# A feed-forward turn in another order: the route at its head, and the last of five chunks in fp32 in the second product

## What is computed

```python
        x_mixed = _mix(x, mix_kernel)
        h = jnp.einsum('bsd,pdm->bspm', x_mixed, W1) + b1
        stacked_paths = jnp.einsum('bspm,pmd->bspd', h, W2) + b2
        scores = jnp.tanh(x_mixed @ Wo1 + bo1) @ Wo2 + bo2
        idx = jnp.argmax(scores, axis=-1)
        weights = jax.nn.one_hot(idx, P, dtype=stacked_paths.dtype)
        collapsed = jnp.einsum('bspd,bsp->bsd', stacked_paths, weights)
        return _layernorm(x + collapsed, gamma, beta)
    ...
    x = x + 0.5 * _L0_ffn_ref(_layernorm(x, axis=-1), ...)
    x = x + _L0_attn_ref(_layernorm(x, axis=-1), ...)
    x = x + 0.5 * _L0_ffn_ref(_layernorm(x, axis=-1), ...)
```

## Time and profile before

| | |
|---|---|
| median of 3 runs | 1528.1 us (1524.33 to 1539.24) |
| the profiled execution | 1531.81 us, span 1530.0 us |
| busy share of the span | PE 89%, DVE 79%, ACT 61%, POOL 20% |
| phase 0, attention, phase 1 | about 0 to 340, 340 to 1220, 1220 to 1530 us |
| DMA | 82.26 MB, mean 54 GB/s |

### The profile page before, as it was taken

How to read it: one execution, slowest core, us unless ns; L and a number is a source line. 1 busy time by engine, 2 the same in 40 slices (tenths; PEclk the granted TensorE clock), 3 DMA queues, 4 the chain that set the end, 5 groups by cost and what they waited for, 6 DMA issues and landing times.

```text
span 1530.0 us, 25980 instructions
## 1 busy us (share of the span) xinstructions
PE 1359.1 (89%) x7700; PEld 781.4 (51%) x7700; DVE 1215.7 (79%) x2349; ACT 936.8 (61%) x1745; POOL 306.9 (20%) x359
## 2 busy tenths in 40 slices
PE   4889988858999999999968999999998779989985
PEld 2556666544554454545344455454444346656653
DVE  6989999766677677677866767777678769999985
ACT  5656665326567666566855666766666666666642
POOL 2244452332001000000041101000000214444311
PEclk9989999979999999999989999999999879999997
DMA  5143333320000100102110011000103112333221
GB/s 155 43 118 88 90 101 113 90 69 1 28 29 15 41 14 15 32 11 74 37 43 1 28 42 42 0 28 0 42 0 110 56 32 61 103 97 106 61 74 57
DMA packets 86994, 82.26 MB, mean 54 GB/s; under 512 B 8540, under 2 KB 86885, under 8 KB 86885
## 3 DMA queue, kind: packets, MB, share of 16 engines
q1 hardware_dynamic: 86884, 80.91, 17.8%
HBM read 55.43 MB, written 25.46 MB: 53 GB/s over the span
## 4 chain that ended last, share of the span: by engine, by line
PE 62%; DVE 11%; DMA 10%; issue 7%; ACT 6%; SPq 2%; POOL 1%; DVEq 0%; ACTq 0%; POOLq 0%
PE PS L1324 55%; DMA R<-oh_scratch 7%; PE PS L1501 3%; DMA oh_scratch<-oh_t 2%; DVE R L753 2%; PE PS L1389 2%; PE PS L1332 1%; DVE R L770 1%; DVE R L937 1%; SPq L414 1%; SPq L412 1%; ACT oh_t L1113 1%; ACT R L1211 1%; ACT R L1215 1%; ACT R L1174 1%
## 5 line engine op out<-in xcount | busy, mean ns | idle before, releaser
L1324 PE MATMUL PS<-R 128*128 128x512 f16 (+3 forms) x3456 | 713.6, 361 | 27.4 <-DVE R L937 17.3
L1324 PEld LDWEIGHTS PS<-R 128*128 128x128 f16 (+1 forms) x3456 | 326.0, 98 | 392.3 <-DVE R L937 32.0
L1324 PE MATMUL PS<-w_hi,R 128*128 128x256 f16 x1280 | 239.1, 280 | 63.3 <-DVE R L753 63.1
L937 DVE TENSOR_TENSOR R<-R 128x512 f16<-128x512 f32 (+3 forms) x288 | 188.6, 655 | 111.5 <-ACT R L1215 110.3
L1202 ACT ACTIVATE R<-PS 128x512 f32 (+5 forms) x288 | 160.2, 558 | 162.7 <-PE PS L1324 162.2
L1324 PE MATMUL PS<-R,w_hi 128*128 128x512 f16 x640 | 198.0, 392 | 1.6 <-DVE R L747 1.5
L1211 ACT ACTIVATE R<-R 128x512 f32 (+4 forms) x288 | 169.5, 589 | 48.3 <-DVE R L931 46.8
L931 DVE TENSOR_TENSOR R<-R,max_row 128x512 f32 (+4 forms) x288 | 187.1, 650 | 7.7 <-ACT max_row L1248 7.7
L1215 ACT ACTIVATE R<-R 128x512 f16<-128x512 f32 (+3 forms) x288 | 171.1, 594 | 28.6 <-ACT R L1211 2.6
L925 DVE TENSOR_TENSOR run_max<-run_max,R 128x512 f32<-128x512 f32 (+3 forms) x272 | 173.9, 639 | 10.0 <-DVE run_max L925 1.7
L1324 PEld LDWEIGHTS PS<-w_hi,R 128*128 128x128 f16 x1280 | 128.4, 100 | 104.5 <-DVE R L753 77.1
(11 more groups left out here) (109 smaller groups left out, 1555.3 us busy)
## 6 DMA issues: line engine op xcount, KB each, us to landing
R<-x_scratch SPq DMA_DIRECT2D x48, 512.0 KB, 4.5
x_scratch<-R SPq DMA_DIRECT2D x32, 512.0 KB, 3.2
R<-oh_scratch SPq DMA_DIRECT2D x32, 320.0 KB
R<-in_L_attn_x SPq DMA_DIRECT2D x16, 512.0 KB, 5.4
R<-oh_scratch SPq DMA_DIRECT2D x32, 256.0 KB
out<-R SPq DMA_DIRECT2D x16, 512.0 KB, 3.2
R<-in_L_ffn_W SPq DMA_DIRECT2D x2, 288.0 KB
R<-in_L_ffn_W SPq DMA_DIRECT2D x1, 512.0 KB
```

The lines of the kernel that those rows point to most:

```text
L937: v.tensor_tensor(p_lo[:, i * TT + lo:(i + 1) * TT], pf[:, (i % 2) * TT + lo:(i % 2 + 1) * TT], p_hi[:, i * TT + lo:(i + 1) * TT], ALU.sub ...
L1324: ins = t_.matmul(dst, w, xx, start=start and n == 0, stop=stop and n == last, skip_group_check=skip)
```

## The change

- DVE's turn begins with result(t-1) and then the five route steps of tile t+2, with the four bn_stats of tile t+6 placed between them (input_sums becomes input_sum, one bn_stats at a time; the wait for x_in is at the first). The mix and the moments come next, then the masks.
- PE's turn begins with the route's scores; choice comes behind path 0. Chunk 0 of tile t+3 (FIRST = 3) is made near the end of the turn, behind transposed(t+5) and ahead of path 4, where it was chunk 0 of t+2 at the turn's head. ACT's turn begins with scores and has one_hot earlier.
- The last chunk (LAST = 4) is no longer split for the second product (w2_last is written in prepare_second, w2_hi and w2_lo shrink to four chunks): masked_high 2 on ACT and masked_low 2 on DVE go, and path(t, 4) multiplies the fp32 masks by fp32 weights (w2_last), four matmuls of 256 columns in place of twelve in f16. hm has two places for chunk 4; hhi and hlo have four chunks.
- POOL's residual moves from tile t+1 behind the masks to tile t behind o_psum of the tile before, at the head of POOL's turn; result_scale(t-1) moves to its end.
- mask_in becomes two semaphores, one for even and one for odd tiles. SP's order of transfers in a turn stays as it is.

```diff
@@ -36,8 +36,12 @@
 
 STATS, ROWS, MIX, ROUTE, HIDDEN = 6, 5, 3, 2, 1
 
-GROUPS = ((0, 2), (2, 2), (4, 1))
-GROUP_OF = (0, 0, 1, 1, 2)
+FIRST = ROUTE + 1
+
+GROUPS = ((0, 2), (2, 2))
+GROUP_OF = (0, 0, 1, 1)
+LAST = HC - 1
+
 XBUF = 3
...
@@ -345,14 +350,22 @@
         h_order = []
         for ph in range(2):
             for t in turns():
-                h_order += [(use(ph, t + ROUTE), 0)] if on(t + ROUTE) else []
                 h_order += [(use(ph, t + HIDDEN), c) for c in range(1, HC)] if on(t + HIDDEN) else []
+                h_order += [(use(ph, t + FIRST), 0)] if on(t + FIRST) else []
         h_bank = {x: i % H_BANKS for i, x in enumerate(h_order)}
         h_before = {x: h_order[i - H_BANKS] if i >= H_BANKS else None for i, x in enumerate(h_order)}
...
+
+        def masked_chunk(t, c, n=1):
+
+            return cols(hm, (c + (t % 2 if c == LAST else 0)) * TT, n * TT)
...
@@ -549,15 +562,14 @@
                     if ph == 0 and t == 0:
                         pool.wait_ge(w2_ready, 1)
                     pool.wait_ge(n_done, k + 1)
-                    pool.wait_ge(hm_done, HC * k + 4)
+                    if t >= 1:
+                        pool.wait_ge(o_psum, k)
                     g.tensor_tensor(rows4(x_rows(t)), rows4(x_rows(t)),
                                     beta_b[:, :].unsqueeze(1).to_broadcast([P, SUB, D]), ALU.add).then_inc(xb_done, 1)
 
                 def turn(t):
-                    if on(t - 1):
-                        result_scale(t - 1)
-                    if on(t + HIDDEN):
-                        residual(t + HIDDEN)
+                    if on(t):
...
@@ -566,6 +578,8 @@
                                    (n_var, n_eps, n_rstd, n_neg, n_shift))
                     elif first_of(ph, t):
                         first_scales(0, first_of(ph, t))
+                    if on(t - 1):
+                        result_scale(t - 1)
 
...
@@ -716,12 +732,15 @@
                 v.memset(chunk(mask, 1, 0)[0:DM, :], 0.0).then_inc(edges_set, 1)
                 dve.wait_ge(edges_set, ph + 1)
 
-                def input_sums(t):
+                def input_sum(t, u):
                     n = counted(ph, t)
-                    dve.wait_ge(x_in[t % NT], 16 * loads(ph, t))
-                    if n >= 2:
-                        dve.wait_ge(n_shift, n - 1)
-                    row_sums(X, t % NT * SUB * D, rows_set(ph, t), n_stat)
+                    if u == 0:
+                        dve.wait_ge(x_in[t % NT], 16 * loads(ph, t))
+                        if n >= 2:
+                            dve.wait_ge(n_shift, n - 1)
+                    ins = v.bn_stats(st[:, rows_set(ph, t), u, :], cols(x_rows(t), u * D, D))
+                    if u == SUB - 1:
+                        ins.then_inc(n_stat, 1)
 
...
@@ -793,11 +812,13 @@
                 def masked(t, c):
 
                     g = use(ph, t)
-                    at = cols(hm, c * TT, TT)
-                    if c in (0, 2, 4) and g >= 1:
-                        dve.wait_ge(hlo_done, 3 * (g - 1) + GROUP_OF[c] + 1)
+                    at = masked_chunk(t, c)
+                    if c in (0, 2) and g >= 1:
+                        dve.wait_ge(hlo_done, len(GROUPS) * (g - 1) + GROUP_OF[c] + 1)
+                    if c == LAST and g >= 2:
+                        dve.wait_ge(o_psum, g - 1)
                     if c == 0:
-                        dve.wait_ge(mask_in, 16 * MASK_LOADS * (g + 1))
+                        dve.wait_ge(mask_in[g % 2], 16 * MASK_LOADS * (g // 2 + 1))
                         dve.wait_ge(hb_done, g + 1)
...
@@ -818,48 +840,34 @@
                         prepare_first()
                     if last:
                         result(t - 1)
+                    for i in range(SUB + 1):
+                        if choice:
+                            route(t + ROUTE, i)
+                        if rows and i < SUB:
+                            input_sum(t + STATS, i)
+                    if mix:
+                        mixed_before(t + MIX, 0)
+                        mixed_before(t + MIX, 1)
+                    if rows:
+                        input_moments(t + STATS)
+                    elif first_of(ph, t):
+                        first_stats(0, first_of(ph, t))
+                    if mix:
+                        mixed_behind(t + MIX, 0)
+                        mixed_behind(t + MIX, 1)
                     if here:
                         masked(t + HIDDEN, 0)
                         masked(t + HIDDEN, 1)
                     if mix:
-                        mixed_before(t + MIX, 0)
-                        mixed_before(t + MIX, 1)
-                    if choice:
-                        route(t + ROUTE, 0)
+                        mixed_low(t + MIX)
                     if here:
                         masked_low(t + HIDDEN, 0)
-                    if choice:
-                        route(t + ROUTE, 1)
-                    if here:
                         masked(t + HIDDEN, 2)
-                    if choice:
-                        route(t + ROUTE, 2)
-                    if mix:
-                        mixed_behind(t + MIX, 0)
-                    if choice:
-                        route(t + ROUTE, 3)
-                    if mix:
-                        mixed_behind(t + MIX, 1)
-                    if choice:
-                        route(t + ROUTE, 4)
-                    if here:
                         masked(t + HIDDEN, 3)
-                    if rows:
-                        input_sums(t + STATS)
-                    elif first_of(ph, t):
-                        first_stats(0, first_of(ph, t))
-                    if mix:
-                        mixed_low(t + MIX)
-                    if here:
                         masked(t + HIDDEN, 4)
-                    if rows:
-                        input_moments(t + STATS)
-                    if here:
                         masked_low(t + HIDDEN, 1)
                     if last:
                         result_scaled(t - 1)
-                    if here:
-                        masked_low(t + HIDDEN, 2)
                     if last:
                         result_added(t - 1)
                     if ph == 0 and t == -ROUTE:
...
@@ -1135,26 +1143,23 @@
                         act.wait_ge(kmix_ready, 1)
                     if ph == 0 and t == -ROUTE:
                         act.wait_ge(w1_ready, 1)
+                    if choice:
+                        scores(t + ROUTE)
                     if mix:
                         middle(t + MIX)
-                    if choice:
-                        scores(t + ROUTE)
-                    if here:
-                        masked_high(t + HIDDEN, 0)
                     if last:
                         squares(t - 1)
+                    if choice:
+                        one_hot(t + ROUTE)
                     if on(t + ROWS):
                         normalised(t + ROWS)
                     if mix:
                         x_high(t + MIX)
-                    if choice:
-                        one_hot(t + ROUTE)
                     if here:
+                        masked_high(t + HIDDEN, 0)
                         masked_high(t + HIDDEN, 1)
                     if on(t + ROWS):
                         transposed(t + ROWS)
-                    if here:
-                        masked_high(t + HIDDEN, 2)
 
                 for t in turns():
...
@@ -1402,29 +1407,35 @@
                     g = use(ph, t)
                     if c == 0 and g >= 1:
                         pe.wait_ge(y_done, g)
-                    pe.wait_ge(hlo_done, 3 * g + GROUP_OF[c] + 1)
-                    high, low = chunk(hhi, t, c), chunk(hlo, t, c)
+                    if c == LAST:
+                        pe.wait_ge(hm_done, HC * g + HC)
+                        rows, w = masked_chunk(t, c), w2_last[:, :]
+                    else:
+                        pe.wait_ge(hlo_done, len(GROUPS) * g + GROUP_OF[c] + 1)
+                        high, low = split_chunk(hhi, t, c), split_chunk(hlo, t, c)
                     for u in range(SUB):
-                        ins = split_product(ps_o[:, u // 2, (u % 2) * D:(u % 2 + 1) * D],
-                                            [((cols(high, u * P, P), cols(low, u * P, P)), (w2_hi[:, c, :], w2_lo[:, c, :]))],
-                                            c == 0 and u % 2 == 0, c == HC - 1, skip=True)
+                        dst = ps_o[:, u // 2, (u % 2) * D:(u % 2 + 1) * D]
+                        if c == LAST:
+                            ins = t_.matmul(dst, cols(rows, u * P, P), w, start=False, stop=True, skip_group_check=True)
+                        else:
+                            ins = split_product(dst, [((cols(high, u * P, P), cols(low, u * P, P)),
+                                                       (w2_hi[:, c, :], w2_lo[:, c, :]))],
+                                                c == 0 and u % 2 == 0, False, skip=True)
```

(23 more changed lines are left out.)

37 lines of the change are left out of this document (22 added, 15 removed).

## The result

The changed kernel takes 1590.67 us (median of 4 runs, 1588.00 to 1593.52) beside 1526.21 us for the one before (4 runs). The ratio is 1.0404, 95% interval 1.0342 to 1.0466: slower, as predicted, but by 64 us between the medians (some 62 by the ratio) instead of 31, and above the upper end of the range (1588). The profiled execution took 1591.11 us with a span of 1589.3, against the 1530.0 of before: +59.3.

What follows compares the result with a forecast made beforehand. DVE was taken as the bound, busy 17.12 of 17.20 us a turn. For each phase +25.1 for loaded turns and -9.4 elsewhere made +15.7, +31.4 for both, so about 1559 us from 1528.1; range 1541 to 1588.

Steps and rivals of the forecast that it cites:

- The load at the head of the turn: In turns 2 to 9 DVE's first bn_stats waits 4.0 us for the rows' load: +25.1 us for each phase.
- the wait of 0.6 for ACT: On DVE between masked 4 and masked_low 1: 0.6 us stay open while it waits for ACT's copy.
- The price of 20.3: Length of a loaded turn, taken between alternating turns of 20.9 and 19.8 us; eight make 162.4 against 137.3 us.
- The clock: PE's clock falls to 0.50 for 5.0 us behind a 3.88 us gap, losing 2.5 us, in every other loaded turn.
- The rival built on it: The clock falls in each loaded turn, 22 us or near it: 1578 us, chance 0.14.
- fp32: PE's path 4 becomes 8 records of 0.25 us, 2.0 us instead of 1.31, +0.7 a turn.
- The dearer rival: Path 4 in fp32 takes 3.0 us, PE's turn 17.1 us: 1578 us, chance 0.10.
- The forecast of 16.1 for an unloaded turn: A turn without a new wait is bound by PE at 16.1 us, where it was 17.16.
- the seven other distances: Result-step distances of each phase outside loaded turns 2 to 9: 101.5 us against 110.9, so -9.4.
- a route step at 3 us in all: On DVE a route step could stand some 0.7 us behind POOL's residual, moving the sum by 3 us.
- The lead-in of phase 0: Turns -6 to 0, a chain from mix to route to mask: taken as 0, -3 to +3 us for each phase.
- The base: Profiled span 1530.0 us, its time 1531.8 being 3.7 above the median, so the +31.4 was added to 1528.1 us.

Runs made afterwards that it cites:

- experiment 1: Changed kernel without the row loads inside the phases, tiles 8 to 15 computed from what lies in the ring: 1520.17 us, ratio 0.9944.
- experiment 2: Changed kernel with the four bn_stats behind masked 3, moments behind masked 4 and POOL's result_scale ahead of norm_scale: 1525.87 us, ratio 0.9993.
- experiment 5: Changed kernel with twelve unread 512-column products in PE's gap ahead of choice in turns 2 to 9: 1581.49 us, ratio 1.0361.
- experiment 3: Changed kernel with SP issuing the load of rows ahead of the store of the result: 1574.24 us, ratio 1.0304.
- experiment 4: Changed kernel's order with the last chunk split as before, masked_high 2 and masked_low 2 back: 1612.73 us, ratio 1.0553.
- experiment 6: Changed kernel with POOL's residual of tile t-1 done in turn t, released by x1_done of the tile before: 1579.53 us, ratio 1.0327.
- kernel 7: Kernel before, in its old order, with only the last chunk in fp32 in the second product: 1509.87 us, ratio 0.9871.
- 10: Kernel before with the fp32 last chunk, POOL's residual(t-1) moved to the turn's head behind x1_done: 1508.30 us, ratio 0.9881.
- 12: Kernel before with the fp32 last chunk, masked 4 and moments ahead of the mix's remainder, hidden 4 ahead of transposed: 1510.46 us, ratio 0.9898.
- experiment 11: Kernel before with the fp32 last chunk, POOL's residual ahead of result_scale and released by masked 0: 1526.85 us, ratio 0.9998.

## Why the prediction was right and wrong

- **The load at the head of the turn**: right, and the largest term. Predicted +50.2 for both phases, measured +53.9; without the loads the kernel is at 1520 (experiment 1), with the statistics late at 1526 (experiment 2). That the sum came so near is in part two misses that offset each other. The wait in phase 1 is 3.6 us in the mean, not 4.0, since the load is issued 0.13 us behind the result step and not 0.55: the result step itself now waits 0.34 for PE, which the prediction had ending 0.4 ahead. Behind the landing the turn then takes 15.7 us, not the 15.1 of the sum: the wait of 0.6 for ACT isn't there, but DVE waits 0.9 for hidden 4 and 0.34 for path 4, and its own work is a little longer. The price of 20.3 was made for phase 1 and used for both; phase 0 had 141.8 us before and not 137.3 (one turn of 21.7 at a clock of 0.76), and its loaded turns are 21.0 in the mean.
- **The clock**: that it falls behind the gap was right, that it does so in every second turn was wrong. The prediction had a late PE shorten its own next gap by 2 us; the gaps are 3.0 to 4.1 us in all loaded turns of phase 1, each of these turns has a clock of 0.92, and they stand at 20.3 to 20.9 us. In phase 0 two have 0.85 and 22.1 and 22.5 us. A fall costs less than the 2.5 us that were taken, 1.78 in the turn shown, so the sum is near: 8 us were in it, 9 by experiment 5. Loaded turns at full clock between the others, with nothing put into the gap, came only with the shorter transfer of experiment 3. The rule of the Trainium skill, TensorE: Matmul & The Clock Gate, section HAM oscillation, is borne out in that the clock did fall in each loaded turn. The rival built on it had the condition right and the price too high: its 22 us a turn are the mean of experiment 4 only (21.94). Its sum has a slip as well: from 20.3 to 22 is 1.7 us and not 1.2, so its own time was 1586 and not 1578.
- **fp32**: path 4 was put at 0.7 us above the split one, and PE's turn grew by 0.45. The dearer rival is out. The forecast of 16.1 for an unloaded turn met 16.31.
- **The step that failed**: the seven other distances, put at -9.4 for each phase. They were +0.3 for both together, 19 us off. The prediction moved the residual "beside result and the statistics" and priced it at nothing. This holds only while DVE ends its turn ahead of PE's path 4. Where DVE ends late, o_psum comes ahead of result_added, and the residual stands in its way (3.2 to 3.3 us for 1.2, in turns 11, 13 and 14 of phase 1 and 14 of phase 0) or in that of result_scaled (3.8 for 1.7, in turns 11 and 13 of phase 0). The rule was in hand, and was applied to a route step at 3 us in all, not to the large instruction at the end. With the residual elsewhere (experiment 6) those distances are 103.3 for the 101.5 predicted in phase 1 and 112.5 for 107.6 in phase 0: 12 of the 19 us come back. The 7 left, most of them in phase 0, stay open.
- **The lead-in of phase 0**: taken as 0, measured +5.0. The trace points to a cause, which no run tried. In the lead-in DVE waits for the route ahead of the mix, which it had behind the mix before:

```profile
31.42 0.20 DVE L796 TENSOR_REDUCE r_max<-PS 128x4 f32<-128x36 f32 x1 [5.61 <-PE PS L1394]
...
33.24 1.41 DVE L751 SCALAR_TENSOR_TENSOR R<-R,kmix 128x512 f32<-128x512 f32 x2
```

  Before, that mix step began at 26.12 and the route step at 30.66. The fp32 chunk is not it: with it and the old order (kernels 7, 10 and 12; 71.9 in 11) the first result step comes at 68.2 to 69.8 us, and with the new order but without it (experiment 4) at 73.1. The attention and phase 1's lead-in moved by 0.1 us together.
- **The base**: the sum was made against one execution of before, 3.7 us above the median shown, then carried to that median. The four executions beside the changed kernel had 1526.21, 2 us less again. So 59.3 us of span are 64 between the medians.

In sum: +54 for +50, 0 for -19, and +5 for 0; the direction hung on the first alone, and its mechanism was the predicted one.

## What to carry over

Where a wait moves to the head of an in-order engine's turn, look at what closes the loop: here the rows' place is freed by the last instruction of one turn and wanted by the third of the next, and the whole transfer is then part of each turn. Here a pass of POOL was free only beside DVE instructions with at most one input tensor in SBUF, and a release that depends on which engine ends first can put it in the worst place, so price both orders of arrival. And an engine busy 99% of a turn (DVE in kernel 7) need not be the only bound: with 1.2 us taken off it the turn stayed, as a loop over two engines had the same length.

## What the runs showed of the hardware

- A 512 KB load that is queued behind a 512 KB store lands in 4.4 to 5.2 us, ahead of it in 4.0 to 4.5 (experiment 3).
- A scalar_tensor_tensor with both tensors in SBUF is held by POOL's pass as a tensor_tensor is: 3.15 us for two in place of 1.41 (experiment 11). Even 36 elements a partition are held, 0.92 for 0.2 us (experiment 2), and four result_scaled take 3.76 for 1.67 (changed kernel).
- With PE gaps of 3.0 to 4.1 us in each turn the clock of the loaded turns of phase 1 was 0.92 in the mean (changed kernel), with 4.1 to 5.7 us 0.88 (experiment 4), and with the gaps filled 1.00 (experiment 5).
- A product of 128x256 in fp32 shows as two records. Eight records took 1.72 us from start to start (1358.30 to 1360.02 in kernel 7), against 1.31 for the twelve f16 products that they replace.
